# A new order of batch 0 (loads, transposes, splits) and products of zeros on TensorE, in a two-layer float32 kernel

## The chip, the cores and the metric

The kernel runs on one core of one Trainium2 chip. The metric is the device time of one execution in microseconds. Of the kernel before three runs were timed: 433.26 (the median), 432.2 and 433.63 us.

## The reference

Two linear layers with adapters, each with a residual, in float32. B is the batch (8), S the rows (256), D the width (1024).

```python
def _L0_cond_ref(hidden_states, W, b, coeff, mask):
    output = jnp.einsum('bsi,oi->bso', hidden_states, W) + b
    sign = (2 * mask - 1).astype(hidden_states.dtype)
    diff = jnp.einsum('bsi,bio->bso', hidden_states, sign)
    return output + diff * coeff[:, None, None]
def _L1_cond_ref(x, adapter_ids, base_weight, base_bias, lora_A_w, lora_B_w):
    result = jnp.einsum('bsd,od->bso', x, base_weight) + base_bias
    A = lora_A_w[adapter_ids]
    Bw = lora_B_w[adapter_ids]
    h = jnp.einsum('bsd,brd->bsr', x, A)
    return result + jnp.einsum('bsr,bor->bso', h, Bw)
x = x + _L0_cond_ref(x, L0_cond_W, L0_cond_b, condB_coeff, mask)
x = x + _L1_cond_ref(x, itok_B_6_15, L1_cond_base_weight, ...)
```

x is 8 x 256 x 1024, the mask 8 x 1024 x 1024 int32, W0 and W1 are 1024 x 1024, each batch has its own adapter (rank 16) out of 32.

## The kernel before

Batch b's first layer is x times (W0 transposed + I + coeff x (2 mask - 1)): the residual is the identity, added to the diagonal blocks of W0 (and of W1 for the second layer) by GpSimd, `eye_w0(c)` and `eye_w1(c)` (L260, L266), before TensorE (PE) transposes them. All products are in float32r, so each operand is split in a high part and a low rest, and a product of two such operands is three products.

The work is a pipeline over 64 chunks n = 8b + c, c a block of 128 of the width between the layers. For each chunk: VectorE (DVE) makes the weight from mask and w0t (`make_w`, L482), ScalarE (ACT) takes its high part (`chunk_hi`, L343), DVE the low (`chunk_lo`, L491). PE runs `layer1(n)` (L614, 8 products of 512 columns in L625 and 8 of 256 in L627, both parts of x side by side) into the PSUM bank L1B + n % 2. ACT and DVE add the two halves and the bias (`half_y`, `make_y`) and split y (`y_parts_hi`, `y_parts_lo`). One chunk later PE runs `adapter_h` (one product, L635) and `layer2` (four quarters of three products, L651 to L653), which accumulates over the eight chunks in banks 0 to 3. After chunk 7 of a batch the h of the adapter is copied (`h_parts_hi` on ACT, `h_parts_lo` on DVE, L385 and L509), and four `finish` products (L657) add h times B and the bias b1. Then `move_z` and `store_z`.

Batch 0 does the weights' preparation beside this. W0, W1, A, B and x of batch 0 are transposed on PE in units of four 128x128 blocks, `turn_unit` (L581, the transposes are L611). A unit fills one PSUM bank; the list `units` (L34) gives kind, chunk, half and bank, and a unit waits until the one before it in its bank has been copied. In the main loop that bank is TB = 7 for all. W0's units are copied by ACT (`copy_w0`), x's, W1's, A's and B's are split into high on ACT (`first_rows_hi`, `split_hi`) and low on DVE (`first_rows_lo`, `split_lo`). In chunk n PE turns w0(n + 2) within layer 1 and w1(n) within layer 2 of chunk n - 1; chunk 0 also turns w0(1), w0(2) and A, chunk 6 turns B. x of later batches is loaded in rows, transposed by DVE (`turn_rows`, L462), split by `rows_hi` and `rows_lo`.

The order of every queue is written out by hand. SP (L220 to L256) issues, in order: ids, w0(0), mask 0, x of batch 0, the coefficients cs, w0(1), mask 1, b0, w1(0), w0(2), mask 2, w1(1), mask 3, b1; then for each n mask n + 4, w1(n + 2), and at set places `move_bias`, `load_bt`, `store_z` and `load_x`. POOL (L291 to L324) makes ident and the constants bt, ht and at, and then issues eye_w0 and eye_w1 between the loads of w0(3) to w0(7) and the sixteen small loads of `load_a` and `load_b`, each of which first reads an adapter number out of id_row. ACT's order is L402 to L451, DVE's L520 to L577, PE's L666 to L721.

## Time and profile before

| | us |
|---|---|
| median of three runs | 433.26 |
| the profiled execution's own time | 435.75 |
| its span | 434.1 |
| PE busy in the span | 409.7 (94%) |
| DVE, ACT, POOL busy | 287.1, 184.6, 24.0 |

The profile is of one execution. Busy times are sums over an engine's instructions; matmuls are pipelined with modelled ends, so two that follow each other can overlap in the rows: the distance between their starts is what one costs. PEld is the weight load beside PE. PEclk is the granted clock of TensorE as a share of 2.4 GHz (its other level is 1.2 GHz). L and a number is a line of the kernel.

### The profile page before, as it was taken

What the parts mean: (1) busy time and instruction counts of PE and PEld (TensorE: products, weight loads), DVE (VectorE), ACT (ScalarE), POOL (GpSimd) and SP (SyncE); (2) the same over time, 40 slices, a digit from 0 to 9 for tenths busy, and PEclk for the clock granted to TensorE, in tenths of its full rate; (3) what the DMA queues carried; (4) which work ended last, traced back from release to release, by engine and by line L of the source; (5) the groups of instructions that cost most, each with busy time, mean ns of one, the idle gap of its engine ahead of it and who ended that gap; (6) DMA issues with size and microseconds to landing.
All of it is one profiled execution on the core that took longest, in us unless ns stands there. A gap on an engine that the chain in (4) does not pass through costs nothing.

```text
span 434.1 us, 5456 instructions
## 1 busy us (share of the span) xinstructions
PE 409.7 (94%) x2049; PEld 342.3 (79%) x2049; DVE 287.1 (66%) x336; ACT 184.6 (43%) x288; POOL 24.0 (6%) x47
## 2 busy tenths in 40 slices
PE   3579998978999999999999999999999999999996
PEld 3568886757888888888888888888888888888884
DVE  0475658676688666776588767776678667866512
ACT  2264555454334533363343434444245433453312
POOL 4325401000000000000000000000000000000000
PEclk9788999899999999999999999999999999999999
DMA  6996796416943399309931595319921894237002
GB/s 224 253 333 195 207 211 179 86 48 151 249 125 94 108 193 222 97 1 233 237 100 50 131 240 150 98 74 209 236 64 36 196 241 120 61 110 169 2 0 97
DMA packets 90845, 63.28 MB, mean 146 GB/s; under 512 B 3515, under 2 KB 84419, under 8 KB 90820
## 3 DMA queue, kind: packets, MB, share of 16 engines
q1 hardware_dynamic: 89588, 59.28, 55.3%
q0 software_dynamic: 1232, 3.67, 2.7%
q8 instruction: 16, 0.26, 0.3%
q14 instruction: 9, 0.07, 0.1%
HBM read 51.39 MB, written 8.39 MB: 138 GB/s over the span
## 4 chain that ended last, share of the span: by engine, by line
PE 88%; DVE 6%; ACT 2%; DMA 2%; issue 1%; SPq 1%; ACTq 0%; DVEq 0%
PE ps L625 27%; PE ps L627 13%; PE ps L652 13%; PE ps L651 13%; PE ps L653 13%; PE ps L635 3%; PE ps L611 3%; PE ps L663 2%; DMA cs<-in_condB_coeff_dram 2%; DVE wm L488 1%; DVE wlo L495 1%; ACT whi L350 1%; DVE w1lo L460 1%; DVE xhl L471 1%; DVE xt L465 0%
## 5 line engine op out<-in xcount | busy, mean ns | idle before, releaser
L625 PE MATMUL ps<-xhl,whi 128*128 128x512 f32 x512 | 187.8, 405 | 2.0 <-DVE wlo L495 1.2
L627 PE MATMUL ps<-xhl,wlo 128*128 128x256 f32 x512 | 145.1, 283 | 0.0
L495 DVE SCALAR_TENSOR_TENSOR wlo<-wm,cs_minus,whi 128x1024 fp32r<-128x1024 f32 x64 | 83.0, 1296 | 53.2 <-ACT whi L350 52.8
L625 PEld LDWEIGHTS ps<-xhl,whi 128*128 128x128 f32 x512 | 97.7, 191 | 25.1 <-DVE wlo L495 1.5
L350 ACT ACTIVATE whi<-wm,cs_minus 128x1024 fp32r<-128x1024 f32 x64 | 73.7, 1151 | 81.7 <-DVE wm L488 80.5
L651 PE MATMUL ps<-w1hi,yhl 128*128 128x512 f32 x256 | 102.0, 398 | 0.0
L652 PE MATMUL ps<-w1lo,yhl 128*128 128x512 f32 x256 | 100.7, 394 | 0.0
L653 PE MATMUL ps<-w1hi,yhl 128*128 128x512 f32 x256 | 100.5, 393 | 0.0
L627 PEld LDWEIGHTS ps<-xhl,wlo 128*128 128x128 f32 x512 | 98.1, 192 | 2.5
L488 DVE SCALAR_TENSOR_TENSOR wm<-wm,cs_twice,w0t 128x1024 f32<-128x1024 int32 x64 | 81.8, 1278 | 11.7 <-ACT w0t L331 11.5
L652 PEld LDWEIGHTS ps<-w1lo,yhl 128*128 128x128 f32 x256 | 48.5, 189 | 10.7
L653 PEld LDWEIGHTS ps<-w1hi,yhl 128*128 128x128 f32 x256 | 48.2, 188 | 10.8
L651 PEld LDWEIGHTS ps<-w1hi,yhl 128*128 128x128 f32 x256 | 48.6, 190 | 7.9
L376 ACT ACTIVATE ysum<-ps,b0col 128x256 f32<-128x256 f32 x64 | 30.0, 469 | 41.2 <-PE ps L627 40.6
L383 ACT ACTIVATE yhl<-ysum 128x256 fp32r<-128x256 f32 x64 | 26.7, 417 | 44.1 <-DVE ysum L502 43.5
L506 DVE TENSOR_TENSOR yhl<-ysum,yhl 128x256 fp32r<-128x256 f32 x64 | 27.1, 424 | 24.0 <-ACT yhl L383 23.7
L502 DVE TENSOR_TENSOR ysum<-ps,ysum 128x256 f32<-128x256 f32 x64 | 26.8, 419 | 19.2 <-ACT ysum L376 19.2
L465 DVE STREAM_TRANSPOSE xt<-xraw 128x1024 f32<-128x1024 f32 x14 | 30.4, 2174 | 0.0
L361 ACT ACTIVATE xhl<-xt 128x1024 fp32r<-128x1024 f32 x14 | 14.9, 1062 | 31.1 <-DVE xt L465 31.1
L635 PE MATMUL ps<-yhl,at 128*128 128x512 f32 x64 | 25.9, 404 | 0.0
L460 DVE TENSOR_TENSOR w1lo<-ps,w1hi 128x512 fp32r<-128x512 f32 x16 | 10.9, 688 | 13.6 <-ACT w1hi L341 13.6
L331 ACT ACTIVATE w0t<-ps 128x512 f32<-128x512 f32 x16 | 9.5, 597 | 22.8 <-PE ps L611 22.8
(50 smaller groups left out, 178.7 us busy)
## 6 DMA issues: line engine op xcount, KB each, us to landing
wm<-in_mask_Bx4096x_ik_dram SPq DMA_DIRECT2D x64, 512.0 KB, 5.8
out_dram<-zst SPq DMA_DIRECT2D x32, 256.0 KB, 2.5
xraw<-in_x_dram SPq DMA_DIRECT2D x28, 256.0 KB, 7.4
w1raw<-_L_cond_base_weight_dram SPq DMA_DIRECT2D x8, 512.0 KB, 6.5
bt<-bhl SPq DMA_DIRECT2D x48, 64.0 KB, 2.9
w0raw<-in_L_cond_W_dram POOLq DMA_DIRECT2D x5, 512.0 KB, 6.7
w0raw<-in_L_cond_W_dram SPq DMA_DIRECT2D x3, 512.0 KB, 9.2
xrows<-in_x_dram SPq DMA_DIRECT2D x2, 512.0 KB, 7.0
```

The source lines that it names most:

```text
L350: nc.scalar.activation(whi[:, n % WS, :, :], wm[:, n % MS, :].rearrange("p (k o) -> p k o", k=KT), ACT.Identity, bias=cs_minus[:, b:b + 1] ...
L376: nc.scalar.activation(ysum[:, n % 2, :], ps[:, L1B + n % 2, S:2 * S], ACT.Identity, bias=b0col[:, n % KT:n % KT + 1]).then_inc(y_half, 1)
L465: nc.vector.transpose(xt[:, :, :].rearrange("p t (n q) -> p n t q", q=Q), xraw[:, :, :].rearrange("p n (i k) -> p n k i", k=KT)[:, :, g * ...
L488: nc.vector.scalar_tensor_tensor(chunk, chunk.bitcast(I32), cs_twice[:, b:b + 1], w0t[:, c, :, :].rearrange("p k o -> p (k o)"), ALU.mult, ...
L495: nc.vector.scalar_tensor_tensor(wlo[:, s, :, :], wm[:, n % MS, :].rearrange("p (k o) -> p k o", k=KT), cs_minus[:, b:b + 1], whi[:, s, :, ...
L506: nc.vector.tensor_tensor(yhl[:, n % 2, S:2 * S], ysum[:, n % 2, :], yhl[:, n % 2, 0:S].bitcast(F32), ALU.subtract).then_inc(y_lo, 1)
L625: nc.tensor.matmul(ps[:, bank, :], whi[:, s, k, :], xhl[:, b % 2, k, :], start=(k == 0), stop=False, skip_group_check=True)
L627: op = nc.tensor.matmul(ps[:, bank, 0:S], wlo[:, s, k, :], xhl[:, b % 2, k, 0:S], start=False, stop=(k == KT - 1), skip_group_check=True)
L635: op = nc.tensor.matmul(ps[:, HB, :], at[:, c, b * 2 * R:b * 2 * R + P], yhl[:, n % 2, :], start=(c == 0), stop=(c == KT - 1))
L651: nc.tensor.matmul(ps[:, Z0 + j, :], hi, w1hi[:, c, cols], start=(c == 0), stop=False)
L652: nc.tensor.matmul(ps[:, Z0 + j, :], hi, w1lo[:, c, cols], start=False, stop=False)
L653: op = nc.tensor.matmul(ps[:, Z0 + j, :], lo, w1hi[:, c, cols], start=False, stop=False)
```

## The change

SP issues no small loads any more: cs, b0, ids and b1 are issued by ACT at its start. SP also takes the loads of w0(3) to w0(7), and loads x of batch 1 in its step 1 instead of 2, x of later batches in step c = 3 instead of 2, B's rows of batch 0 in step 5 instead of 7. POOL fills bt first, waits for ids and issues two of A's loads before eye_w0(0), four before eye_w0(1), and it splits b1 (before: ACT and DVE). B's loads come in two groups of four, behind eye_w0(3) and eye_w1(2).

In batch 0 layer 1 uses one PSUM bank (4), so that the transposes have two, TB = (5, 7), one for each half. w0 is turned one chunk ahead instead of two; A in chunk 1 instead of 0, B in chunk 4 instead of 6. adapter_h(0) runs in chunk 2, after A is split. x of batch 0 goes by halves of the width, and chunk 0 starts after the first half. ACT and DVE follow this order; chunk 9's weight is made at the end of chunk 7, behind the split of w1(7). x of later batches is transposed and split second half first, and layer 1 of a batch waits for both halves at its start.

PE computes nine products of bt's zeros into bank 5 as soon as bt is filled, and ten more between w0(0) and x.

```diff
-    Z0, L1B, HB, TB = 0, 4, 6, 7
+    Z0, L1B, HB, TB = 0, 4, 6, (5, 7)
-    units = [("w0", 0, 0, 0), ("w0", 0, 1, 1), ("x", 0, 0, 4), ("x", 0, 1, 5), ("x", 1, 0, 6), ("x", 1, 1, 7),
...
+    units = [("w0", 0, 0, 0), ("w0", 0, 1, 1), ("x", 0, 0, 2), ("x", 1, 0, 3), ("x", 0, 1, 6), ("x", 1, 1, 7),
+             ("w0", 1, 0, 0), ("w0", 1, 1, 1), ("w1", 0, 0, 2), ("w1", 0, 1, 3)]
     for n in range(1, KT):
+        if n + 1 < KT:
+            units += [("w0", n + 1, h, TB[h]) for h in range(2)]
+        if n == 4:
+            units += [("b", 0, h, TB[h]) for h in range(2)]
+        for h in range(2):
+            units.append(("w1", n, h, TB[h]))
+            if n == 1:
+                units.append(("a", 0, h, TB[h]))
...
+    def l1_bank(n):
+        return L1B if n < KT else L1B + (n + 1) % 2
...
             for n in range(NS):
+                if n + 4 < KT:
+                    load_w0(n + 4)
                 if n + 4 < NS:
                     load_mask(n + 4)
                 if n + 2 < KT:
                     load_w1(n + 2)
+                if n == 1:
+                    load_x(1)
...
             pool.wait_ge(ident_set, 2)
+            pool.wait_ge(ids_in, 16)
+            load_a(range(0, 2))
             eye_w0(0)
+            load_a(range(2, 6))
             eye_w0(1)
+            load_a(range(6, NB))
             eye_w1(0)
             eye_w0(2)
             eye_w1(1)
             eye_w0(3)
+            load_b(range(0, 4))
             eye_w0(4)
             eye_w1(2)
+            load_b(range(4, NB))
             eye_w0(5)
+            pool.wait_ge(b1_in, 16)
+            nc.gpsimd.tensor_copy(b1hi[:, :], b1raw[:, :]).then_inc(bias_hi, 1)
...
             eye_w1(3)
...
 (ACT)
+            for n in range(1, KT):
+                if n + 1 < KT:
+                    copy_w0(n + 1, 0)
+                    copy_w0(n + 1, 1)
+                if n == 4:
+                    split_hi("b", 0, 0)
+                    split_hi("b", 0, 1)
+                if n == 5:
+                    rows_hi(1, 1)
+                if n == 7:
+                    rows_hi(1, 0)
+                    chunk_hi(8)
+                half_y(n)
+                if n < 7:
+                    chunk_hi(n + 1)
+                y_parts_hi(n)
+                for h in range(2):
+                    split_hi("w1", n, h)
+                    if n == 1:
+                        split_hi("a", 0, h)
+                if n == 7:
+                    chunk_hi(9)
 (DVE)
+            for n in range(1, KT):
+                make_w(n + 1)
+                if n == 4:
+                    split_lo("b", 0, 0)
+                    split_lo("b", 0, 1)
+                if n == 7:
+                    rows_lo(1, 0)
+                    chunk_lo(8)
+                make_y(n)
+                if n < 7:
+                    chunk_lo(n + 1)
+                y_parts_lo(n)
+                if n == 5:
+                    rows_lo(1, 1)
+                for h in range(2):
+                    split_lo("w1", n, h)
+                    if n == 1:
+                        split_lo("a", 0, h)
+                if n in (3, 6):
+                    turn_rows(1, 2 - n // 3)
+                if n == 7:
+                    make_w(9)
+                    chunk_lo(9)
 (PE, in layer1)
+                    elif n < KT:
+                        pe.wait_ge(y_made, n)
...
+                    if n == KT:
+                        pe.wait_ge(parts_lo, parted(number["w1", KT - 1, 0]))
 (PE)
+            def idle_products(count):
+                for _ in range(count):
+                    nc.tensor.matmul(ps[:, TB[0], :], bt[:, 0:P], bt[:, 0:HALF], start=True, stop=True)
+            pe.wait_ge(consts_set, 1)
+            idle_products(9)
             pe.wait_ge(ident_set, 2)
+            pe.wait_ge(b0_in, 16)
+            nc.tensor.transpose(ps[:, L1B, 0:KT], b0row[:, :], ident[0:KT, 0:KT]).then_inc(b0_turned, 1)
             turn_unit("w0", 0, 0)
             turn_unit("w0", 0, 1)
+            idle_products(10)
+            for g in range(2):
+                for st in range(ST):
                     turn_unit("x", st, g)
...
+                if n + 1 < KT:
+                    layer1(n, range(0, 2))
+                    turn_unit("w0", n + 1, 0)
+                    layer1(n, range(2, 4))
+                    turn_unit("w0", n + 1, 1)
+                    if n == 2:
+                        pe.wait_ge(parts_lo, parted(number["a", 0, 1]))
+                        adapter_h(0)
...
                 if m == 0:
...
+                    layer2(0, 0, 0)
+                    turn_unit("w1", 1, 0)
+                    layer2(0, 0, 1)
+                    turn_unit("a", 0, 0)
+                    layer2(0, 1, 0)
+                    turn_unit("w1", 1, 1)
+                    turn_unit("a", 0, 1)
+                    layer2(0, 1, 1)
```

## Rows read from the trace of the kernel before

**Rows 1.** windows: length, busy PE, PEld, DVE, ACT, POOL, PEclk, DMA share, GB/s

```profile
0.00:17.26 17.26, 5.69 (x26) 5.03 (x26) 5.21 (x8) 5.68 (x8) 7.59 (x19) 0.96 0.86 237
17.26:27.60 10.34, 9.10 (x50) 8.20 (x49) 3.13 (x5) 4.20 (x8) 3.83 (x7) 0.74 1.12 286
27.60:40.18 12.58, 10.69 (x46) 8.77 (x46) 7.58 (x10) 6.80 (x13) 4.74 (x9) 0.73 0.80 246
40.18:71.59 31.41, 31.10 (x181) 25.92 (x180) 22.13 (x26) 18.44 (x31) 7.17 (x13) 1.00 0.78 197
71.59:83.05 11.46, 9.51 (x46) 7.40 (x45) 7.65 (x9) 5.28 (x8) 0.67 (x1) 0.85 0.63 162
83.05:100.60 17.55, 14.06 (x72) 11.12 (x71) 14.11 (x17) 8.43 (x16) 0.00 (x0) 1.00 0.15 37
100.60:434.10 333.50, 329.58 (x1637) 275.83 (x1635) 227.25 (x262) 135.74 (x210) 0.00 (x0) 1.00 0.55 133
```

**Rows 2.** PE's waits in 0 to 101 us: us in total, times, longest

```profile
PE ps L611 <- POOL w0raw L264: 5.5, 1, 5.5
```

**Rows 3.** PE's timeline in batch 0: start, us, work, [idle before and its releaser]

```profile
76.32 0.66 PE L611 MATMUL ps<-ident,bsort 128*128 128x128 f32 x4 [1.95 <-DVE bhl L460]
...
77.65 0.63 PE L635 MATMUL ps<-yhl,at 128*128 128x512 f32 x1
...
98.91 0.93 PE L663 MATMUL ps<-bt,ht 128*128 128x512 f32 x3 [1.78 <-ACT ht L394]
```

**Rows 4.** timelines of DVE and PE where batch 3 begins

```profile
185.54 1.23 DVE L471 TENSOR_TENSOR xhl<-xt,xhl 128x1024 fp32r<-128x1024 f32 x1
...
188.74 0.39 PE L625 MATMUL ps<-xhl,whi 128*128 128x512 f32 x1
...
191.55 0.39 PE L635 MATMUL ps<-yhl,at 128*128 128x512 f32 x1
```

**Rows 5.** PE's timeline at the end of chunk 2

```profile
46.38 0.40 PE L653 MATMUL ps<-w1hi,yhl 128*128 128x512 f32 x1
...
46.80 0.66 PE L611 MATMUL ps<-ident,w1raw 128*128 128x128 f32 x4
```

**Rows 6.** the page's costliest groups, whole run: busy us, mean ns; idle before, releaser

```profile
L488 DVE SCALAR_TENSOR_TENSOR wm<-wm,cs_twice,w0t 128x1024 f32<-128x1024 int32 x64 | 81.8, 1278 | 11.7 <-ACT w0t L331 11.5
...
L350 ACT ACTIVATE whi<-wm,cs_minus 128x1024 fp32r<-128x1024 f32 x64 | 73.7, 1151 | 81.7 <-DVE wm L488 80.5
...
L495 DVE SCALAR_TENSOR_TENSOR wlo<-wm,cs_minus,whi 128x1024 fp32r<-128x1024 f32 x64 | 83.0, 1296 | 53.2 <-ACT whi L350 52.8
...
L460 DVE TENSOR_TENSOR w1lo<-ps,w1hi 128x512 fp32r<-128x512 f32 x16 | 10.9, 688 | 13.6 <-ACT w1hi L341 13.6
...
L331 ACT ACTIVATE w0t<-ps 128x512 f32<-128x512 f32 x16 | 9.5, 597 | 22.8 <-PE ps L611 22.8
...
L502 DVE TENSOR_TENSOR ysum<-ps,ysum 128x256 f32<-128x256 f32 x64 | 26.8, 419 | 19.2 <-ACT ysum L376 19.2
```

**Rows 7.** timelines of SP, DVE and POOL in the head

```profile
3.55 0.44 SPq L225 DMA_DIRECT2D cs<-in_condB_coeff_dram  x1
...
11.07 0.17 DVE L521 TENSOR_SCALAR cs_twice<-cs 128x8 f32<-128x8 f32 x1 [11.07 <-DMA cs<-in_condB_coeff_dram]
...
4.85 0.45 POOL L264 TENSOR_TENSOR w0raw<-w0raw,ident 128x128 f32<-128x128 f32 x1 [1.44 <-DMA w0raw<-in_L_cond_W_dram]
...
6.37 0.66 POOL L282 DMA_DIRECT2D abraw<-in_L_cond_lora_A_w_dram  x1 [1.06 <-issue]
...
7.55 0.49 POOL L282 DMA_DIRECT2D abraw<-in_L_cond_lora_A_w_dram  x1 [0.53 <-issue]
```

**Rows 8.** the page's DMA issues: count, KB each, median us to landing

```profile
bt<-bhl SPq DMA_DIRECT2D x48, 64.0 KB, 2.9
```

**Rows 9.** POOL's timeline, one of B's eight loads

```profile
43.93 0.53 POOL L289 DMA_DIRECT2D abraw<-in_L_cond_lora_B_w_dram  x1 [0.72 <-issue]
```

**Rows 10.** groups by line, 17.26 to 100.6 us, the low half of b1

```profile
L556 DVE TENSOR_TENSOR b1lo<-b1raw,b1hi 1x1024 fp32r<-1x1024 f32 x1 | 1.2, 1206 | 0.0
```

More of the change, by code:

```diff
@@ L249, in _ @@
                     load_bt(b)
-                if c == 2 and b + 1 < NB:
+                if c == 3 and 0 < b < NB - 1:
                     load_x(b + 1)
@@ L319, in _ @@
                                   abraw[:, :].rearrange("p (b o r) -> p o b r", b=NB, o=KT)).then_inc(b_sorted, 1)
+            eye_w0(6)
             eye_w1(4)
@@ L501, in make_y @@
                 row = ysum[:, n % 2, :]
-                nc.vector.tensor_tensor(row, ps[:, L1B + n % 2, 0:S], row, ALU.add).then_inc(y_made, 1)
+                nc.vector.tensor_tensor(row, ps[:, l1_bank(n), 0:S], row, ALU.add).then_inc(y_made, 1)
             def y_parts_lo(n):
@@ L518, in move_z @@
                 nc.vector.tensor_copy(zst[:, 2 * st + 1, :], ps[:, Z0 + 2 * st + 1, :]).then_inc(z_moved_dve, 1)
+            dve.wait_ge(b0_turned, 1)
+            nc.vector.tensor_copy(b0col[:, :], ps[:, L1B, 0:KT]).then_inc(b0_moved, 1)
             dve.wait_ge(coeff_in, 16)
@@ L524, in _ @@
             make_w(0)
-            first_rows_lo(0, 0)
             chunk_lo(0)
-            first_rows_lo(0, 1)
-            first_rows_lo(1, 0)
-            first_rows_lo(1, 1)
-            dve.wait_ge(b0_turned, 1)
-            nc.vector.tensor_copy(b0col[:, :], ps[:, TB, 0:KT]).then_inc(b0_moved, 1)
+            for g in range(2):
+                for st in range(ST):
+                    first_rows_lo(st, g)
             make_w(1)
@@ L534, in _ @@
             chunk_lo(1)
-            for n in range(KT):
-                if n == 6:
+            y_parts_lo(0)
+            split_lo("w1", 0, 0)
+            split_lo("w1", 0, 1)
+            for n in range(1, KT):
+                make_w(n + 1)
+                if n == 4:
                     split_lo("b", 0, 0)
-                make_w(n + 2)
-                if n == 6:
                     split_lo("b", 0, 1)
-                if n > 0:
-                    make_y(n)
-                if n == 0:
-                    split_lo("a", 0, 0)
-                    split_lo("a", 0, 1)
-                split_lo("w1", n, 0)
-                split_lo("w1", n, 1)
-                y_parts_lo(n)
-                if n in (5, 7):
-                    rows_lo(1, (n - 5) // 2)
-                chunk_lo(n + 2)
-                if n in (4, 6):
-                    turn_rows(1, (n - 4) // 2)
-                if n == 1:
-                    dve.wait_ge(bias_hi, 1)
-                    nc.vector.tensor_tensor(b1lo[:, :], b1raw[:, :], b1hi[:, :].bitcast(F32),
-                                            ALU.subtract).then_inc(bias_lo, 1)
+                if n == 7:
[4 more added lines that the diff above has]
+                    chunk_lo(n + 1)
+                y_parts_lo(n)
+                if n == 5:
+                    rows_lo(1, 1)
[8 more added lines that the diff above has]
+                    chunk_lo(9)
             for n in range(KT, NS):
@@ L562, in _ @@
                 if c in (5, 7) and b + 1 < NB:
-                    rows_lo(b + 1, (c - 5) // 2)
+                    rows_lo(b + 1, 1 - (c - 5) // 2)
                 if n + 2 < NS:
@@ L615, in layer1 @@
                 b, c = divmod(n, KT)
-                bank = L1B + n % 2
+                bank = l1_bank(n)
                 s = n % WS
```

154 lines of the change are left out of this document (57 added, 97 removed).

## The prediction

> **What bounds the kernel now.** Read by stage first [rows 1]: the borders are the starts of a chunk's first L625 product, written T0 (17.26 us, chunk 0) to T9 (100.60), with T1 27.60, T2 40.18, T6 71.59, T7 83.05. After T9 PE is busy 329.6 of 333.5 us at full clock, so batches 1 to 7 are TensorE's own time, 333.5 / 7 = 47.6 us each. Batch 0, with its head, takes 100.6 us. What is to be had lies there, in three forms: the head, in which PE is busy 5.7 of 17.3 us; waits; and half clock. The granted clock was 0.74, 0.73 and 0.85 in three stages; at two levels, 1 and one half, that is 2 x 0.26 x 10.34 = 5.4 us, 6.8 us and 3.4 us at 1.2 GHz, each costing up to half of itself. The longest wait of PE in it is for the identity add before the first transposes, 5.5 us [rows 2]. Two more stand singly [rows 3]: 1.95 us for B's split, with the adapter product behind it taking 0.63 us instead of the 0.39 of [rows 4] (half clock after the gap), and 1.78 us for h, after which no slow stretch came.
>
> **Prices.** Layer 1 of a chunk takes 191.55 - 188.74 = 2.81 us [rows 4]. A steady chunk takes (47.6 - 0.9 for four finish products) / 8 = 5.84, so adapter and layer 2 are 3.03, 0.23 a product. Chunks 2 to 5 take 31.41 / 4 = 7.85 [rows 1] with four transposed units each. In it is one wait of 0.19: the last L653 starts at 46.38, is done with its 0.23 at 46.61, and the next unit starts at 46.80 [rows 5]. So a unit costs (7.85 - 5.84 - 0.19) / 4 = 0.45. The vector steps [rows 6]: make_w 1.28, chunk_hi 1.15, chunk_lo 1.29, copy_w0 0.60 and split_hi the same, split_lo 0.69 (0.6 to 0.65 back to back), y steps 0.42. Steps of 1.28 that follow each other come 1.2 apart.
>
> **The head.** Before, DVE stood until 11.07 for the coefficients, issued at 3.55 on SP behind 2 MB [rows 7]: 7.5 us. They, b0, ids and b1 move to ACT's queue. The third of them, ids, is issued at about 2.0 (0.44 each from 0.9). Its flight is not shown; bounds: 2.9 us, the median of bt's 64 KB pieces [rows 8], and the 7.5 of cs. I take 2.9, since ACT's queue holds nothing large: 4.9. But POOL now waits for ids and issues two adapter loads before it adds the identity to w0(0). From the end of that add at 5.30 to the end of the second load at 8.04 is 2.7 us [rows 7]; as the id read could overlap the add I take 3.0. So the add ends at 4.9 + 3.0 + 0.45 = 8.35, 3.05 us later than before. Two units at half clock (0.9 each), the last copy (0.6) and about 0.3 of handovers follow, 2.7 in all: make_w(0) starts at 11.05, hardly before the old 11.36. Then 1.28 + 1.15 + 1.29 and two row splits (only half 0 of x is needed now, and no b0 transpose stands behind it): T0 = 16.1, gain 1.2. The nine products of zeros lie in idle time; the ten between w0(0) and x (2.3 us at full, 4.6 at half clock) run beside make_w and chunk_hi. With the last of the four x units that T0 needs they end near 15 if the clock rises on the way, so they cost nothing; if it does not, T0 moves to about 17. What they buy: chunk 0 at full clock, which was half for 5.4 us.
>
> What moves without a price: bt's memset stands ahead of ident's, but POOL stood 1.44 us for w0(0) [rows 7] and now stands for ids. The five later W0 loads go from POOL to SP (POOL is free of five issues) and stand ahead of a mask load each; their wait is for a unit turned early in the chunk, and the data is used two chunks or more later. x(1), 1 MB, goes ahead of w0(6) and w1(4): at the 286 GB/s of [rows 1] that is 3.7 us, and both have a chunk of 7.6 us in hand. load_bt(0) waits for B's split, now in chunk 4, ahead of mask 10, first used in chunk 8. DVE's b0col copy stands ahead of everything on its queue; b0 is issued before ids, so it has landed first. If the cover of the early loads goes, DMA share 1.12 and 0.80 [rows 1] say where: chunks 0 and 1.
>
> **Chunk 0 to 1.** w0(1) is turned by T0 + 2.3; copy 3.0, make_w(1) 4.3, chunk_hi 5.45, chunk_lo 6.75. PE's own work is 2.81 + 4 x 0.45 = 4.6, so PE waits 2.15 and T1 = T0 + 6.75 = 22.85. Before 10.34 us; chunk 0 sheds four units (w0(2), A).
> **Chunk 1** takes the four units of w0(2) and w1(1) and both of A: 2.81 + 2.75 + 6 x 0.45 = 8.25. But a(0,0) goes into the bank that w1(1,0) filled 1.1 us before, and its split stands behind chunk_lo(2) and y_parts_lo on DVE: free at T1 + 7.75, where PE arrives at 5.5. Wait 2.25; then a(0,1) directly behind w1(1,1) waits for its hi and lo, 1.3. T2 = T1 + 11.75 = 34.6 (before 12.58 us).
> **Chunks 2 to 5.** The second bank removes the 0.19: 7.6. Chunk 2 has one adapter product more (0.23), chunk 4 B's two units (0.9). POOL's queue is what costs: load_b waits for A's last transpose (T1 + 11), and four loads, a cadence of 1.25 [rows 9] behind the first, which needs 1.6 with its id read (5.30 to 6.37 alone is 1.07 [rows 7]), then eye_w0(4) and eye_w1(2) at 0.45: 33.85 + 1.6 + 3.75 + 0.53 + 0.9 = 40.65. PE wants w1(2) after layer 1, two units, two adapter products and a quarter, T2 + 4.85 = 39.45: wait 1.2. Then four loads, eye_w0(5) and the bias pair (two passes over 1024 elements, 1.2 each by the DVE row [rows 10]) stand before eye_w1(3): 40.65 + 5.9 + 0.45 + 2.4 + 0.45 = 49.85, wanted at T3 + 4.6 = 48.2, wait 1.6. Below, these waits are nothing if PE is late anyhow; above, 1 us more if POOL is slow on one partition. move_bias waits behind w1(5)'s load on SP and lands about when B's split asks. rows_lo(1,1) delays w1(5)'s splits: 0.3 and, in chunk 6, 0.7. The four: 9.0 + 9.2 + 8.6 + 7.9 = 34.7 against 31.4, T6 = 69.3.
> **Chunk 6** loses B and its 1.95 wait: 7.6 + 0.7 = 8.3 (before 11.46): T7 = 77.6.
> **Chunks 7 and 8** get worse. L1(8) now needs the bank of w1(7,0), whose split stands behind chunk_lo(8) and y(7): T7 + 8.6, with PE there at 6.75, wait 1.85. Chunk 9 is now made after the W1 splits instead of before: make, hi, lo of 9 and then of 10 run in series before h_parts_hi and h_parts_lo, which release finish at T8 + 8.5 where PE arrives at 5.1: a wait of 3.4 instead of 1.78. T9 = T7 + 8.6 + 10.2 = 96.4 (before 17.55 us).
> **Later batches.** x(b+1) is issued one chunk later, and its halves swapped. The second half was split by 185.54 + 1.23 = 186.8, and L1 of the next batch starts at 188.74 [rows 4]: 1.9 us of cover, so asking for both halves at the start costs nothing. Freed ids, b0 and b1 issues on SP only let its loads go earlier.
>
> **The sum.** T0 16.1, then 6.75 + 11.75 + 34.7 + 8.3 + 18.8 = 80.3: T9 96.4 against 100.6, gain 4.2. As a check, PE's own time is 9 x 2.81 + 8 x 3.03 + 0.9 + 34 x 0.45 = 65.7 and the waits named are 2.15 + 3.55 + 1.2 + 1.6 + 0.3 + 0.7 + 1.85 + 3.4 = 14.75, together 80.45. Half clock takes some back: gaps of 2.15, 2.25 and 3.4 us are like the 1.95 us one that was followed by 3.4 us of half clock and unlike the 1.78 us one that was not. A spell costs 1.7; in chunks 0 and 1 PE has slack that swallows part. I charge one, 1.8. Gain 2.4 us. The profiled execution took 435.75 with a span of 434.1; it lies 2.5 above the median 433.26, so I take the difference off the median: **430.9** (profiled span 431.7).
>
> **A rule against it.** The trace's small load on SP's queue needed 7.5 us behind 2 MB. The Trainium skill says in *Trainium Kernel Development and Optimization*, Key Constraints, that queues of several issuing engines run on the same 16 DMA engines and that issuing from several "only saves the sequencer's issue time". By it ids would land no sooner than cs did; no row here shows ACT's queue, and the same skill's *DMA: Bandwidth & Descriptors* (Queues, rings and completion order) has each engine take turns between the queues, which would favour my 2.9. The sum here needs neither.
>
> **Rivals.** A change smaller than 0.3% (1.3 us) can't be told from none.
> *1. Ids arrive late: slower.* With the 7.5 us of cs, ids land at 9.5, the first identity add ends at 13.0, T0 is 20.7, everything behind moves by 4.6: 430.9 + 4.6 = 435.5. It decides from a landing past 7.3 (all gain gone). For: DMA share 0.86 in the head [rows 1] and the only small row. Against: that row stood in one queue behind 2 MB. 0.18. (The rule above would give just this.)
> *2. The clock stays high and POOL keeps up: much faster.* No spell (1.8), no POOL waits (2.8), T0 up to 1 us sooner: 430.9 - 5.6 = 425.3. For: products of zeros leave PE warm at T0 and PE late anyhow hides POOL. Against: the gaps inside chunks 0, 1 and 8 hold no such products. 0.22.
> *3. No change.* The zeros don't raise the clock (T0 17, chunk 0 at half: but its 2.15 us of slack hides most), two more spells at 1.7 in chunks 1 and 8 paid in full, a slow bias pair on POOL: the 4.2 turn to about 0, 433.0. 0.20.
> *Forecast*: 429.3 to 432.0, 0.40.
>
> **Numbers.** Range 425.3 to 435.5 by the rivals, 425.0 to 436.0. Faster 0.22 + 0.38 = 0.60; same 0.02 + 0.19 = 0.21; slower 0.18 + 0.01 = 0.19.
>
> **What would show it.** In the new profile: first transposes near 8.4 instead of 5.45; make_w(0) near 11; first layer 1 product near 16 and taking 0.40 us, not the 0.63 of half clock; waits on DVE's split before A's units (2.2 and 1.3); waits on POOL's w1raw before w1(2) and w1(3); T9 near 97 to 98 with a wait of over 3 us on ht. Wrong if the first transposes start past 11, if PE waits for POOL by more than 2 us at one place, or if batches 1 to 7 no longer take 47.6 us each.

## The result and the profile after

The changed kernel is slower: 441.91 us (median of 4 runs, 439.61 to 442.44) against 433.44 (4 runs, 432.2 to 436.56), a ratio of 1.017 with a 95% interval of 1.012 to 1.022. The forecast was 430.9 with a range up to 436.0: wrong in sign and outside its range.

The profiled execution took 439.61 us, the fastest of its four. The one of before took 435.75, slower than its median. So the two profiles differ by 3.8 us of span (437.9 against 434.1) and the medians by 8.5; the profile shows the places, but not the full price. The clock is part of it: of 95 later executions of the kernel before, the 36 with a mean granted clock below 0.98 took 435.8 us on average, the 15 at 0.995 or above 432.6. The profiled one (0.978) is of the first kind, and all executions of the changed kernel lie at 0.975 to 0.984.

The windows of the changed kernel, with borders at T0, T1 and so on as in [rows 1] (length, then busy us of PE, PEld, DVE, ACT, POOL, then PEclk, DMA share, GB/s):

```profile
0.00:17.48 17.48, 10.86 (x45) 8.81 (x45) 4.33 (x8) 5.69 (x8) 7.57 (x19) 0.90 0.89 244
17.48:24.58 7.10, 4.82 (x32) 4.22 (x33) 4.03 (x6) 4.10 (x7) 1.57 (x2) 1.00 1.15 257
24.58:39.19 14.61, 10.88 (x53) 8.81 (x54) 7.12 (x11) 5.41 (x9) 0.92 (x2) 0.79 0.96 281
39.19:47.85 8.66, 8.30 (x47) 6.95 (x46) 4.21 (x6) 4.16 (x7) 5.15 (x9) 0.96 1.04 262
47.85:58.27 10.42, 7.77 (x46) 6.50 (x45) 6.79 (x6) 4.33 (x8) 8.70 (x9) 1.00 0.54 167
58.27:67.37 9.10, 8.69 (x55) 7.37 (x54) 8.35 (x9) 6.30 (x10) 1.85 (x2) 1.00 0.40 119
83.45:104.35 20.90, 15.22 (x71) 12.15 (x70) 15.79 (x18) 9.38 (x16) 0.00 (x0) 0.93 0.21 64
104.35:437.90 333.55, 329.61 (x1637) 275.98 (x1635) 227.10 (x262) 135.79 (x210) 0.00 (x0) 1.00 0.54 132
```

Batches 1 to 7 are what they were, 333.55 us for 333.50. All of the loss is ahead of T9, which is 104.35 instead of 100.60. Chunk 0 is the one gain, 7.10 us instead of 10.34 and at full clock. Chunk 1 is 14.61 instead of 12.58, chunk 3 10.42 instead of about 7.8, chunk 4 9.10, chunks 7 and 8 together 20.90 instead of 17.55.

PE's waits in 0 to 110 us, the counterpart of [rows 2] (us in total, times, longest), name the owners:

```profile
PE ps L627 <- DVE w1lo L476: 4.4, 3, 2.3
PE ps L627 <- POOL w0raw L278: 3.3, 1, 3.3
PE ps L689 <- ACT ht L405: 3.3, 1, 3.3
PE ps L627 <- POOL w1raw L284: 3.0, 2, 2.6
PE ps L649 <- DVE w1lo L476: 2.4, 1, 2.4
PE ps L649 <- DVE wlo L511: 2.3, 1, 2.3
```

The chain of waits gives the head, and PE's timeline the places that answer to [rows 3]:

```profile
1.91 3.83 DMA id_row<-in_itok_B_dram
```

```profile
9.59 0.47 PE L627 MATMUL ps<-ident,w0raw 128*128 128x128 f32 x1 [3.31 <-POOL w0raw L278]
...
17.48 0.47 PE L649 MATMUL ps<-xhl,whi 128*128 128x512 f32 x1 [1.33 <-DVE xhl L494]
...
32.66 0.78 PE L627 MATMUL ps<-ident,abraw 128*128 128x128 f32 x4 [2.31 <-DVE w1lo L476]
...
33.67 0.63 PE L678 MATMUL ps<-w1lo,yhl 128*128 128x512 f32 x1
...
36.99 1.11 PE L627 MATMUL ps<-ident,abraw 128*128 128x128 f32 x4 [1.41 <-DVE w1lo L476]
...
55.30 0.63 PE L627 MATMUL ps<-ident,w1raw 128*128 128x128 f32 x4 [2.65 <-POOL w1raw L284]
...
101.27 1.57 PE L689 MATMUL ps<-bt,ht 128*128 128x512 f32 x3 [3.30 <-ACT ht L405]
102.64 0.63 PE L677 MATMUL ps<-w1hi,yhl 128*128 128x512 f32 x1
```

Both of A's waits (2.31, 1.41) and the one for h (3.30) are close to the forecast's. What it did not price is the product of 0.63 us behind them: half clock, from 32.66 to about 40 and again at 101 to 104. The gap alone does not decide it. In e12 (below) the same gap of 2.31 us stands at the same place, and the product behind it runs at full clock:

```profile
32.55 0.66 PE L627 MATMUL ps<-ident,abraw 128*128 128x128 f32 x4 [2.31 <-DVE w1lo L476]
...
33.28 0.39 PE L678 MATMUL ps<-w1lo,yhl 128*128 128x512 f32 x1
```

POOL's timeline around chunk 3, the counterpart of [rows 9]:

```profile
46.63 0.54 POOL L297 DMA_DIRECT2D abraw<-in_L_cond_lora_B_w_dram  x1 [0.61 <-issue]
49.47 0.54 POOL L297 DMA_DIRECT2D abraw<-in_L_cond_lora_B_w_dram  x1 [2.30 <-issue]
50.02 0.47 POOL L278 TENSOR_TENSOR w0raw<-w0raw,ident 128x128 f32<-128x128 f32 x1
50.42 1.03 POOL L323 CAST b1hi<-b1raw 1x1024 fp32r<-1x1024 f32 x1
51.53 3.21 POOL L325 TENSOR_TENSOR b1lo<-b1raw,b1hi 1x1024 fp32r<-1x1024 f32 x1
54.71 0.44 POOL L284 TENSOR_TENSOR w1raw<-w1raw,ident 128x128 f32<-128x128 f32 x1
55.10 2.04 POOL L328 COPY bsort<-abraw 128x1024 f32<-128x1024 f32 x1
```

The identity add of w1(3), forecast for the end of 49.85, starts at 54.71. Ahead of it stand the eighth of B's loads, which POOL issues after 2.30 us of idle time where the others come after 0.6, and the low half of b1 with 3.21 us instead of the 1.2 taken from DVE's row [rows 10].

### The profile page after: what moved, and what is told of

Read it like the earlier page. It is cut to its first block, busy times and chain, and to the rows that moved or that the text cites. A ratio compares the mean times of both kernels' runs of the same rounds, so it can differ in the third digit from the quotient of the medians.

```text
span 437.9 us, 5497 instructions
## 1 busy us (share of the span) xinstructions
PE 411.6 (94%) x2068; PEld 343.9 (79%) x2068; DVE 287.9 (66%) x335; ACT 184.4 (42%) x287; POOL 27.6 (6%) x44
## 4 chain that ended last, share of the span: by engine, by line
PE 82%; DVE 7%; ACT 3%; issue 3%; POOL 2%; POOLq 1%; DMA 1%; ACTq 0%; DVEq 0%
PE ps L649 25%; PE ps L651 12%; PE ps L678 12%; PE ps L677 12%; PE ps L679 12%; PE ps L659 3%; PE ps L627 3%; DVE wm L504 2%; PE ps L689 2%; DVE wlo L511 2%; ACT whi L361 2%; DVE w1lo L476 1%; DMA id_row<-in_itok_B_dram 1%; POOL b1lo L325 1%; ACT w0t L342 1%
## 5 line engine op out<-in xcount | busy, mean ns | idle before, releaser
L649 PE MATMUL ps<-xhl,whi 128*128 128x512 f32 x512 | 185.1, 400 | 6.0 <-DVE w1lo L476 2.4
L649 PEld LDWEIGHTS ps<-xhl,whi 128*128 128x128 f32 x512 | 96.6, 189 | 29.1 <-issue 4.3
L651 PEld LDWEIGHTS ps<-xhl,wlo 128*128 128x128 f32 x512 | 96.9, 189 | 2.6
L522 DVE TENSOR_TENSOR yhl<-ysum,yhl 128x256 fp32r<-128x256 f32 x64 | 28.0, 438 | 24.5 <-ACT yhl L394 24.2
L487 DVE TENSOR_TENSOR xhl<-xt,xhl 128x1024 fp32r<-128x1024 f32 x14 | 17.2, 1225 | 0.0
```

What stands on the lines that cost most here:

```text
L522: nc.vector.tensor_tensor(yhl[:, n % 2, S:2 * S], ysum[:, n % 2, :], yhl[:, n % 2, 0:S].bitcast(F32), ALU.subtract).then_inc(y_lo, 1)
L649: nc.tensor.matmul(ps[:, bank, :], whi[:, s, k, :], xhl[:, b % 2, k, :], start=(k == 0), stop=False, skip_group_check=True)
L651: op = nc.tensor.matmul(ps[:, bank, 0:S], wlo[:, s, k, :], xhl[:, b % 2, k, 0:S], start=False, stop=(k == KT - 1), skip_group_check=True)
```

## The experiments

Theory after the result: the loss is the sum of waits in batch 0 that the new order brings, on POOL's queue (chunk 3), on the banks of A (chunk 1) and on the order of DVE and ACT (chunks 7 and 8), with half clock behind some of them. Rivals: the products of zeros or the clock; and, as a whole, that the loads of batch 0 are the bound, so that what is won at one place is lost at the next. Unless another kernel is named, each experiment is the changed kernel with one edit. Ratios are to the kernel before, run beside it, with 95% intervals; differences in microseconds between two variants are of medians, and where a variant has only four runs, those under about 2.5 us are not clear of the noise.

### The zeros: e1 and e10

```diff
-            idle_products(9)
-            idle_products(10)
```

e1 leaves out these products, whose result nobody reads.

> The changed kernel without its 19 products of zeros. Theory O (the loss is made by the order of the queues in chunks 1, 3, 4, 7 and 8, and the zeros only raise the clock of chunk 0): the first chunk and the transposes of x run at half clock for 3 to 6 us again, T1 comes 0.5 to 2 us later, the waits behind it stay, in all 0 to 3 us slower than the changed kernel (441 to 445 us). Theory Z (the zeros themselves cost the time, by holding TensorE or by bringing the clock down later): the kernel comes back to 434 to 438 us.

442.21 us, 1.019 (1.012 to 1.025). The window of chunk 0 (length, busy times, PEclk third from the end):

```profile
17.29:25.98 8.69, 6.39 (x32) 5.65 (x32) 4.02 (x6) 4.09 (x7) 1.32 (x3) 0.80 1.13 273
```

It is 8.69 us instead of 7.10 at a clock of 0.80 instead of 1.00, so the zeros do raise the clock of chunk 0 (nine of the ten profiles of the changed kernel and its one-edit variants with the zeros have 7.10 to 7.12 us there, e5 has 7.53). At the end 0.3 us are seen, with intervals too wide to exclude a gain of 1 to 2 us. The opposite, e10, gives the kernel before nineteen such products (bt filled ahead of ident):

> The kernel before with only the 19 products of zeros and bt's memset first. Theory O: chunk 0 at full clock, T1 1 to 2 us earlier, of which the split waits of chunk 1 take part: 0 to 2 us faster than the kernel before. Theory Z (zeros cost): slower by 1 us or more.

434.04 us, 1.000 (0.997 to 1.002). Its chunk 0 is 9.57 instead of 10.34, but that is not the zeros' doing. e11 (below), the kernel before without zeros, has 9.55, and in both the first products of chunk 0 run at half clock:

```profile
18.11 0.63 PE L625 MATMUL ps<-xhl,whi 128*128 128x512 f32 x1
```

```profile
18.03 0.63 PE L630 MATMUL ps<-xhl,whi 128*128 128x512 f32 x1
```

(e10, then e11.) In e10 PE stands 5.36 us between the transposes of x and T0, in the changed kernel 1.33, and the clock that the zeros raised is gone by T0. So e10 shows that the zeros do no harm; it does not show what a full clock in chunk 0 of the kernel before would be worth, and no run does. (PEclk is no sure guide here: e11's chunk 0 reads 1.00. The times of single products are.)

### POOL's queue: e2, e7, e12, e17

e2 puts b1's split behind the identity add that PE waits for:

```diff
+            eye_w1(3)
             pool.wait_ge(b1_in, 16)
             ... (b1hi, b1lo)
-            eye_w1(3)
```

> The changed kernel with one edit on GpSimd: the identity add of w1(3) stands before the split of the bias b1 instead of behind it. Theory O: TensorE's wait of 2.65 us for that add goes, and with it the slow VectorE steps beside the 3.2 us subtraction move elsewhere: T4 2 to 3 us earlier, in all 1.5 to 3 us faster than the changed kernel (439 to 440.5 us). Rival D (what is late in chunk 3 is a transfer, w1(3) or B, and the add only stands in its place in the queue): less than 0.5 us.

438.51 us, 1.011 (1.004 to 1.018): 3.4 us below the changed kernel by the medians, 2.5 by the ratios, whose intervals overlap. The trace is clearer. The wait in chunk 3 is gone (8.35 us for 10.42), though chunk 4 takes 10.24 for 9.10. So the split is one cause.

e7 puts eye_w0(4), eye_w1(2) and b1's split ahead of all of B's loads:

> The changed kernel with GpSimd's adds of w0(4) and w1(2) and the split of b1 ahead of all eight loads of B. Theory O: the waits for GpSimd's adds (3.0 us together) go; the split of b1 now lies in the 12 us in which GpSimd had nothing to do, where it stretches one or two VectorE steps of chunk 1 by about 1 us; the eighth B load, which stood 2.3 us, may still hold w1(3). In all 2 to 4 us faster than the changed kernel (438 to 440). Rival D: the eighth load waits for transfers, and takes up what was freed: less than 1 us.

437.77 us, 1.007 (1.003 to 1.010). B's first loads no longer cost chunk 2 anything (7.83 us), but PE waits 3.2 us in chunk 3: the eighth load comes 5.78 us of idle time after the seventh, although the first seven start earlier. That made the eighth load a suspect of its own. e12 moves the two adds and b1's split up as in e7, and eye_w1(3) ahead of the eighth load:

```diff
             eye_w0(3)
-            load_b(range(0, 4))
             eye_w0(4)
             eye_w1(2)
-            load_b(range(4, NB))
-            eye_w0(5)
             ... (b1hi, b1lo)
+            load_b(range(0, NB - 1))
+            eye_w0(5)
             eye_w1(3)
+            load_b(range(NB - 1, NB))
```

> The changed kernel with GpSimd's order so that b1 is split in its idle stretch and the adds of w0(4), w1(2), w0(5) and w1(3) all stand ahead of the eighth load of B. Theory R (GpSimd can't issue B's eighth load before the seventh has landed, and what stands behind it waits; that, with the split of b1, is the whole loss of chunk 3): no wait for GpSimd's w1raw adds, T4 minus T3 7.6 to 7.9 us instead of 10.4, the eighth issue still near 50; B is sorted at about 54 and may hold chunk 4 for 0 to 1.5 us. 2.5 to 4.5 us faster than the changed kernel (437 to 439). Rival (the eighth load waits for GpSimd's own work, not for landings): the eighth issue comes within 1.5 us of the seventh.

436.36 us, 1.004 (1.001 to 1.007): 5.5 us below the changed kernel with this order as the only edit. The add of w1(3) is done by 46.3 instead of 55.15, and T2, T3 and T4 are:

```profile
45.84 0.46 POOL L284 TENSOR_TENSOR w1raw<-w1raw,ident 128x128 f32<-128x128 f32 x1
```

```profile
36.95 0.40 PE L649 MATMUL ps<-xhl,whi 128*128 128x512 f32 x1
...
44.77 0.39 PE L649 MATMUL ps<-xhl,whi 128*128 128x512 f32 x1
...
52.37 0.39 PE L649 MATMUL ps<-xhl,whi 128*128 128x512 f32 x1
```

Chunks 2 and 3 take 7.82 and 7.60 us, and PE is busy in all of it. T9 is 98.92, 5.4 earlier. Of this 2.8 us come from chunk 3 and 0.8 from chunk 2; 2.1 come from chunk 1 (12.47 at a clock of 1.00), where A's two waits are the same (2.31 and 1.41) and only the half clock behind them is missing. e7's profile has no half clock there either (12.48), but other executions of e7 and e12 have mean clocks down to 0.969 and 0.975, so that part is not shown to be the order's doing.

Why the eighth load waits was asked with e17, which gives POOL's queue an eighth more room for descriptors (1024 to 1152 where the kernel is set up):

> The changed kernel, with nothing but the room for the descriptors of GpSimd's queue raised from 1024 to 1152. Theory (the room holds seven of B's loads, and the eighth is issued when the first ones of the group give it back): the eighth load of B is issued 1.15 us behind the seventh instead of 2.84, with 0.6 us idle ahead of it instead of 2.3; eye_w1(3) comes 1.7 us earlier and the wait of layer 2 in chunk 3 shrinks by up to that; median 440 to 442. Rival (GpSimd or its descriptor writing is only slow at that point, or waits for landings for another reason): the gap ahead of the eighth stays at 2 us or more and the times are those of the changed kernel.

440.22 us, 1.011 (1.008 to 1.015), and POOL's timeline:

```profile
49.99 0.53 POOL L297 DMA_DIRECT2D abraw<-in_L_cond_lora_B_w_dram  x1 [2.80 <-issue]
```

The gap stays, so the room as set there is not shown to be the reason (no run has more). What the runs do show is that the gap goes with how long B's loads take to land, once that is more than about 3.5 us. Idle time ahead of the eighth, and median landing time: 2.19 and 2.3 us before; 2.30 and 3.8 after; 2.80 and 4.4 in e17; 3.86 and 5.2 in e12; 5.78 and 6.1 in e7; 5.20 and 7.6 in e13. Below that it stays near 2 us: in e8 (below) the loads land in 2.5 instead of 3.8 us and the gap is 2.25. The eighth may be issued when some earlier one has landed; that is not shown, and it is no rule for every eighth load. A's eight loads, of the same size on the same queue, take longer to land (6.8 us in the changed kernel, 7.2 before), and the idle time ahead of their eighth is 1.00 and 0.65 us.

### A's bank, the first identity add, x: e3, e5, e8

e3 turns a(0,0) into the unused bank of h, and a(0,1) into the first transpose bank:

```diff
-                units.append(("a", 0, h, TB[h]))
+                units.append(("a", 0, h, (HB, TB[0])[h]))
```

> The changed kernel with A's first half transposed into bank 6, which is free, and its second half into bank 5. Theory O: the waits of 2.31 and 1.41 us in chunk 1 fall to under 1 us together, and as the gap that ended in half clock is gone, chunk 1 runs at full clock: T2 minus T1 falls from 14.6 to 9 to 10.5 us, in all 3 to 5 us faster (437 to 439 us) if what follows does not take it back; GpSimd's queue with B's loads starts earlier too, so it should not. Rival: the wait moves to w0(3), which follows in bank 5, or to GpSimd's add of w1(2), and less than 1 us is left.

440.41 us, 1.015 (1.008 to 1.022). Chunk 1 takes 10.81 us for 14.61, 3.8 less. All of it and more goes in chunk 3, 15.86 for 10.42:

```profile
PE ps L627 <- POOL w1raw L284: 7.1, 2, 6.6
```

```profile
43.59 0.53 POOL L297 DMA_DIRECT2D abraw<-in_L_cond_lora_B_w_dram  x1 [0.61 <-issue]
49.51 0.53 POOL L297 DMA_DIRECT2D abraw<-in_L_cond_lora_B_w_dram  x1 [5.39 <-issue]
```

The seventh load is issued 3 us earlier than in the changed kernel, the eighth at the same 49.5. PE is only sooner at the wait, and the 1.5 us between the medians is within the noise.

e5 puts eye_w0(0) ahead of the wait for ids and all of A's loads:

```diff
+            eye_w0(0)
             pool.wait_ge(ids_in, 16)
-            load_a(range(0, 2))
-            eye_w0(0)
-            load_a(range(2, 6))
+            load_a(range(0, 6))
```

> The changed kernel with the identity add of w0(0) ahead of the wait for ids and of A's loads. Theory O: the add, at 9.07 us behind two loads in the changed kernel, comes back to about 4.8, the first transposes start at about 6, right behind the nine products of zeros, and T0 falls from 17.5 to 13.5 to 15 us. Of these 2.5 to 4 us the transfers of chunk 1 (w1(1) landed at 25.6) and B's loads take some back: T9 1.5 to 4 us earlier. Rival D (transfers bound chunks 0 to 2): T1 or T2 hardly move, less than 0.7 us is left at T9.

442.02 us, 1.014 (1.010 to 1.019). T0 is 14.84 instead of 17.48, T2 36.55 instead of 39.19, and chunk 3 14.52 instead of 10.42. Again the same wait (5.2 us) takes it all.

e8 loads x of batch 1 in step 2, as before, instead of 1:

> The changed kernel with the load of x(1), 1 MB, issued in SP's step 2 as before the change. Rival D (the early load of x(1) lies in front of B's rows, w0(6) and w1(4), and lets B's loads land late, so that the eighth cannot be issued): that load's idle time falls from 2.3 us, B's landing from 3.8 towards the 2.3 us of the kernel before, and the wait for w1(3)'s add falls by 1 to 2 us. Theory O (only the work in GpSimd's own queue counts): the wait stays within 0.5 us and so does the time.

440.26 us, 1.011 (1.006 to 1.016), 1.7 below the changed kernel by the medians, but its profile has a span of 439.4 and chunk 4 at 10.55. No clear gain, and no sooner eighth load.

### Chunks 7 and 8: e4, e6, e11

e4 puts chunk 8's layer 1 into the bank that the transposes do not use (`L1B + n % 2`), so that it need not wait for w1(7,0):

> The changed kernel with chunk 8's layer 1 in bank 4 and chunk 9's in bank 5, so that chunk 8 waits for y(7) instead of the split of w1(7). Theory S (chunks 7 and 8 are bound by the series of VectorE and ScalarE steps that ends in the h parts, not by the bank): T8 comes 1.5 to 2 us earlier, the wait for h grows by the same, T9 is the same within 0.3 us. Rival B (the bank is what costs): T9 1.5 to 2 us earlier, and the kernel faster by that.

441.41 us, 1.018 (1.010 to 1.026). Layer 1 of chunk 8 starts 2 us earlier (chunk 7 is 7.20 us for 9.21) and its h wait grows by nearly the same:

```profile
PE ps L689 <- ACT ht L405: 5.1, 1, 5.1
```

So what bounds chunk 8 is the series of DVE's and ACT's steps for chunks 9 and 10. e6 takes chunk 10's three steps to behind h and y:

```diff
-                if n + 2 < NS:
+                if n + 2 < NS and n != KT:
                     chunk_hi(n + 2)
...
                 y_parts_hi(n)
+                if n == KT:
+                    chunk_hi(n + 2)
 (DVE the same, with make_w and chunk_lo)
```

> The changed kernel with the weight of chunk 10 made behind the h parts of batch 0 instead of ahead of them, on ScalarE and VectorE. Theory S (the series of steps of chunks 9 and 10 releases the finish products late): the wait for h (3.3 us in the changed kernel, 1.7 us in three variants) goes, T9 minus T8 falls from 10.3 (11.7 with a slow stretch) to about 8.6, and the kernel is 1.5 to 3 us faster. Rival: chunk 10's weight is then late for its layer 1, and the gain is given back at T10: less than 0.5 us.

439.61 us, 1.010 (1.006 to 1.015). Chunk 8 is 6.78 us instead of 11.69, and the h wait is gone; 4.9 us in the profile, of which 2.3 are seen in the median (T2 was later there, 41.40 for 39.19). Two things make the 4.9 too large a price for the wait. The half clock behind it is in it: in e1, e2, e3 and e8, where the slow products come before the wait and shorten it to 1.7 us, chunk 8 takes 10.3. And in every profile with this edit PE waits 1.0 to 1.1 us for h at the end of the next batch, in none without it. The likely reason, not traced, is that what is behind chunk 10's weight on DVE stays late until then.

e11 makes the same edit in the kernel before, and no other:

> The kernel before with only chunk 10 made behind the h parts of batch 0. Theory S: the 1.78 us wait for h goes and T9 minus T8 falls from 9.77 to about 8; 1.0 to 1.8 us faster than the kernel before. Rival: chunk 10 comes late or the wait moves to h's own four steps: no change.

433.47 us, 0.999 (0.996 to 1.002). Its chunk 8 is 7.74 for 9.77, but 1.0 us of that comes back as the same wait one batch later, and the median moves by 0.4 against the kernel before, inside the noise.

### Together: e9, e13, e16, e14, e18, e19

e9 has the edits of e3, e5, e6 and e12:

> The changed kernel with four edits: the add of w0(0) first, A in free banks, GpSimd's adds before B's eighth load with b1 split in its idle stretch, chunk 10 behind the h parts. If the causes found add up (2.6 us at T0, 3.8 in chunk 1, 2.8 in chunk 3, 3.5 in chunk 8), T9 is 104.35 - 12.7 = 91.7; B's loads, which can't go much earlier, may give back 1 to 3 us in chunk 4: T9 92 to 95 against 100.6 before, so 6 to 8 us faster than the kernel before (427 to 430). Rival (transfers bound the start at 1.1 DMA share): T2 not below 35, T9 above 98, no faster than the kernel before.

434.06 us, 1.000 (0.998 to 1.003). T4 is 48.62 us, 7.2 earlier than before (55.78), and then chunk 4 takes 17.61:

```profile
PE ps L631 <- POOL bsort L327: 6.1, 1, 6.1
```

```profile
51.06 0.55 POOL L297 DMA_DIRECT2D abraw<-in_L_cond_lora_B_w_dram  x1 [5.56 <-issue]
56.74 1.03 POOL L327 COPY bsort<-abraw 128x1024 f32<-128x1024 f32 x1 [5.13 <-DMA abraw<-in_L_cond_lora_B_w_dram]
```

B is there at 56.7 and no sooner, so chunk 4 is too early to ask for it. e13 is e9 with B asked for in chunk 5 (B's units, their splits, x(1)'s last half and the first load of bt one chunk later):

```diff
-        if n == 4:
+        if n == 5:
             units += [("b", 0, h, TB[h]) for h in range(2)]
```

> The combined kernel (e9) with B transposed and split in chunk 5 instead of 4, and with the last half of x(1) and bt's first load one chunk later too. Theory (the causes add; B's last load is late by itself and only the place where B is asked for decides): no wait on bsort above 1 us, chunk 4 about 7.6 us instead of 17.6, chunk 5 about 8.6, T9 near 90 to 92 us, a median of 424 to 427 us, ratio 0.98. Rival (what is removed in one place comes back in the next, as in e3, e5 and e9, because the transfers of batch 0 as a whole bound it): another wait of 4 us or more on a weight or mask appears in chunks 4 to 8, T9 stays at 98 to 101 and the median at 433 to 435.

435.31 us, 1.001 (0.999 to 1.003), a miss. The wait on bsort is gone, but one of 5.0 us stands in its place, on the identity add of w1(4), which is queued behind bsort:

```profile
50.48 0.55 POOL L297 DMA_DIRECT2D abraw<-in_L_cond_lora_B_w_dram  x1 [5.20 <-issue]
56.25 1.03 POOL L327 COPY bsort<-abraw 128x1024 f32<-128x1024 f32 x1 [5.21 <-DMA abraw<-in_L_cond_lora_B_w_dram]
57.25 0.44 POOL L278 TENSOR_TENSOR w0raw<-w0raw,ident 128x128 f32<-128x128 f32 x1
57.66 0.44 POOL L284 TENSOR_TENSOR w1raw<-w1raw,ident 128x128 f32<-128x128 f32 x1
```

e16, e13 without the zeros:

> e13 without the nineteen products of zeros. Theory (they raise the clock of chunk 0, and nothing later hides it now): chunk 0 takes 8.7 us instead of 7.1 and the median is 1 to 2 us above e13. Rival (as in e1, the later chunks wait for transfers and take it back): within 0.5 us of e13.

435.66 us, 1.002 (1.000 to 1.004). The difference of 0.35 cannot be told from none. It is a weak test, since this wait, which ends at about the same time in both, hides what comes earlier; in e18, where no such wait is left, the zeros were not taken out. e14 adds e4's bank to e13:

> e13 with chunk 8's layer 1 in the bank that the transposes don't use, as in e4. Theory (chunk 9's and 10's vector steps bound chunk 8, so an earlier start of layer 1 in chunk 8 alone gives little; with h ahead of chunk 10 in e13 this bound is gone): 1 to 1.5 us faster than e13. Rival: as in e4 the wait only moves to the next place: within 0.5 us of e13.

432.91 us, 0.996 (0.994 to 0.998), 2.4 below e13. With the series of chunk 10 out of the way (e6's edit), the bank that was worth nothing in e4 is worth its 2 us. e18 is e14 with two adds ahead of the wait for B:

```diff
+            eye_w0(6)
+            eye_w1(4)
             pool.wait_ge(b_in, 16 * NB)
             nc.gpsimd.tensor_copy(bsort...)
-            eye_w0(6)
-            eye_w1(4)
```

> e14 with the identity adds of w0(6) and w1(4) ahead of the copy bsort on GpSimd. Theory (queueing on GpSimd: w1(4) is issued at 40.9 us on SP, and has the 8.8 us median of its kind to land, so it is there by 51): w1(4)'s add runs at 51.3, PE's wait of 4.7 us in chunk 4 is gone or under 0.5, chunk 4 takes about 8 us instead of 13.95, and the half clock behind the wait goes with it; T9 near 91 and a median of 427 to 429, ratio 0.985. Rival (w1(4) lands late too, or the 4.7 us come back at bsort in chunk 5): a wait of 3 us or more in chunks 4 to 6, the median within 1.5 us of e14.

**426.0 us** (425.63 to 427.62, 6 runs), 0.981 (0.978 to 0.984): faster than both kernels, 6.9 us below e14 by the medians, 6.4 by the ratios. POOL's timeline, and chunk 4 in the windows, 7.58 us where e14 had 13.95:

```profile
51.52 0.55 POOL L297 DMA_DIRECT2D abraw<-in_L_cond_lora_B_w_dram  x1 [4.88 <-issue]
52.10 0.47 POOL L278 TENSOR_TENSOR w0raw<-w0raw,ident 128x128 f32<-128x128 f32 x1
52.75 0.46 POOL L284 TENSOR_TENSOR w1raw<-w1raw,ident 128x128 f32<-128x128 f32 x1 [0.18 <-DMA w1raw<-_L_cond_base_weight_dram]
56.91 1.11 POOL L329 COPY bsort<-abraw 128x1024 f32<-128x1024 f32 x1 [3.71 <-DMA abraw<-in_L_cond_lora_B_w_dram]
```

```profile
49.78:57.36 7.58, 7.58 (x46) 6.57 (x45) 6.25 (x7) 4.21 (x8) 1.93 (x4) 1.00 0.99 286
```

B's loads are as late as ever, but the add that PE needs in chunk 4 no longer stands behind the wait for the last of them. POOL waited 0.18 us for w1(4) to land, so the weights' loads are close behind. T9 is 90.71, 13.6 us ahead of the changed kernel and 9.9 ahead of before. No single product of 512 columns from T0 to the end took over 0.50 us: with no wait of PE above 2 us, no half-clock spell came. Part of the gain is this clock: against the executions of the kernel before that also ran at 0.995 or above (432.6), 6.6 of the 8.8 us are left. What e6's edit gives back is still in it, a wait of 1.1 us for h in the next batch. e19 is e18 with x of batch 1 one step later:

> e18 with x of batch 1 loaded in step 2, as in the kernel before, instead of step 1. Theory (the traffic of 36 to 56 us no longer sets a wait of PE): within 1 us of e18. Rival (x in the middle of the weights' loads is what makes B's last load and w1 late, SP standing 4.5 us at one issue): B's eighth load is issued at 47 instead of 50.8 and the median is 1 to 3 us below e18.

428.57 us, 0.987 (0.984 to 0.989): 2.6 slower than e18, and B's eighth load is issued at 53.05, later and not sooner. Both guesses miss: in e18, loading x(1) early pays. In the changed kernel itself (e8) it was not seen to.

## Why the prediction was wrong

T9 was to be 96.4 (97 to 98 with one half-clock spell charged) and is 104.35. By its own steps, measured less forecast: T0 +1.4, chunk 0 +0.35, chunk 1 +2.9, chunk 2 -0.3, chunk 3 +1.2, chunk 4 +0.5, chunk 5 -0.3, chunk 6 +0.2, chunk 7 +0.6, chunk 8 +1.5: together 8.0, of which 1.8 was charged. The forecast failed in three steps: the one charge for half clock, the waits added chunk by chunk although they end in one queue on POOL, and a median taken from a profile.

- **The head** (T0 17.48 for 16.1). The mechanism is right: POOL waits for ids. Their flight was 3.83 us where I took 2.9, between the bounds of 2.9 and 7.5; the two adapter loads with their id reads took 3.3 for 3.0. Rival 1 did not come: ids did not need the 7.5 us of cs in [rows 7], and cs itself, now first on ACT's queue, took 5.7. That is no case against the rule that I had named (the Trainium skill, *Trainium Kernel Development and Optimization*, Key Constraints: more queues save only issue time). Before, ids went first on SP's queue, at 0.87, and POOL, free at 5.30, issued A's first load after 1.06 us, the same as in e9 and e18, where POOL asks later than ids land; so ids were there by then, 4.4 us after their issue at most. What both cases have in common is that nothing large was issued ahead of it on its queue. e5 shows that 2.6 us of head was to be had by the order on POOL.
- **Chunk 1** missed most. Its waits were as forecast (2.31 and 1.41 for 2.25 and 1.3), but the step "I charge one, 1.8" for the whole of batch 0 was too small: chunk 1 took 14.61 us with half clock from 32.66 and 12.47 with the same waits without it (e12), so half clock costs 2.1 there, and a second spell, at 101, 1.4 in chunk 8 (11.69 for 10.3). The other 0.7 of chunk 1 is PE's own work, 8.75 us for the 8.25 of the sum, and 0.2 in the waits. I had likened these gaps to the 1.95 us one that was followed by half clock, and should have put each into the bounds. Not every gap brings one: behind those of 2.65 us at 55.30 and 2.38 at 92.66 the products take 0.39 to 0.40 us, and the gap of 2.31 was followed by half clock here and by full clock in e12.
- **Chunk 3** (POOL's queue). The wait was priced at 1.6 us and measured 2.65. From A's last transpose (done at 38.1) to the end of w1(3)'s add (55.15) POOL took 17.05 us; the sum had 16.0 (33.85 to 49.85). The mis-sized term is b1's pair: 2.4 us by DVE's row, 4.25 on POOL (50.49 to 54.74). "1 us more if POOL is slow" was too small a bound. The last four loads took 5.3 us for 5.9 even with the 2.30 us gap ahead of the eighth, so there the sum was saved by a second error: the eighth load was not known to come late. It costs little as long as all is late; once PE or B's loads come earlier, the waits behind it are 3 to 7 us (e3, e5, e7, e9). e2 and e12 show what the order of this queue is worth: 3.4 and 5.5 us by the medians; in the trace of e12, 3.6 us lie in chunks 2 and 3.
- **Chunks 7 and 8**: h wait 3.3 for 3.4, w1lo wait 2.38 for 1.85. e4 and e6 confirm the series that I named. Only the half clock was left out. They do not show the full price of the wait: moving chunk 10 costs 1.1 us a batch later.
- **The zeros** did what rival 2 wanted, a full clock in chunk 0, and 7.10 us is near the 6.75 of the sum. But e1 shows nothing of it at the end, to within 1 to 2 us: in the changed kernel later waits take it. What half clock in chunk 0 cost the kernel before stays open, since e10's zeros did not remove it.
- **Profile and median.** Subtracting the gain from the median assumed that the profiled execution sits the same way in both. It lay 2.5 above the median used before (433.26; the 95 later executions have 434.5) and 2.3 below it after, which makes 4.8 of the 11.0 us by which the forecast missed; 6.2 are in the profile's sum (a span of 437.9 for 431.7). The clocks in the section on the result show why such a difference is no constant: with them the executions of the kernel before move by 3.2 us, and its profiled one was of the slower kind.
- **What the forecast had no step for**: that the order on POOL is one chain through batch 0. I added waits chunk by chunk; e3, e5 and e9 show that PE arriving sooner only waits longer, since B's eighth load is issued at 49.2 to 51.1 us although the seventh comes at 43.6 to 44.0 (46.63 and 49.47 in the changed kernel). That is the rival that was missing, and it turns any gain ahead of chunk 3 into a longer wait.

## What to carry to other kernels

On an engine that both issues loads and does small steps that others wait for, put each step ahead of every wait and every load that its consumer does not need; two such reorderings on POOL, with no work removed, went with 5.5 us (e12, of which chunks 2 and 3 explain 3.6) and 6.9 us (e18 against e14) of the 15.9 between the changed kernel and e18. Judge a wait by whether its end is fixed: if a gain ahead of it does not come through, look for the load or the queue that ends it, and move that or the need. And where a gap of TensorE of 2 us or more is forecast, put the half clock that may follow into the bounds once for each gap, not once for the kernel; the same gap brought it in one execution and not in another.
